# First layer item's projections, rotary products and GpSimd parts placed in the last two cross-attention iterations

## The reference

```
x = x + xattn(layernorm(x), ctx_768)            # 8 heads of 64, 77 context rows
h = layernorm(x)
for l in range(2):                               # 2 layers
    s = shift_token(h)                           # second half of the channels one token later
    q, k, v = split(s @ wqkv[l])                 # 256 -> 3 x 512
    q, k = l2norm(q) * qs, l2norm(k) * ks
    q, k = rotary_xpos(q, k)
    h = h + local_attention(q, k, v) @ wo[l]     # windows of 128, look back one window
    s = layernorm(shift_token(h)) * lg + lb
    a, g = split(s @ w1[l] + b1[l])
    h = h + (a * gelu(g)) @ w2[l] + b2[l]
x = x + h
```

## Time and profile before

| | us |
|---|---|
| median of 3 runs | 1458.46 |
| lowest and highest | 1457.38, 1459.85 |
| the profiled execution | 1456.24 |
| its span, first to last instruction | 1454.1 |
| mean granted TensorE clock | 0.995 |

### The profile page before, as it was taken

How to read it: one execution, slowest core, us unless ns; L and a number is a source line. 1 busy time by engine, 2 the same in 40 slices (tenths; PEclk the granted TensorE clock), 3 DMA queues, 4 the chain that set the end, 5 groups by cost and what they waited for, 6 DMA issues and landing times.

```text
span 1454.1 us, 32911 instructions
## 1 busy us (share of the span) xinstructions
PE 1404.0 (97%) x11652; PEld 1251.9 (86%) x11652; DVE 1099.9 (76%) x3067; ACT 936.7 (64%) x2662; POOL 761.4 (52%) x576
## 2 busy tenths in 40 slices
PE   7989999898999999999999999999999999999988
PEld 6888888787888888888888888888888888888877
DVE  5677677456888878777877878888778888887874
ACT  4777766345666666666666677666666666666662
POOL 1112112155666666665555667765566655555653
PEclk8999999999999999999999999999999999999999
DMA  6122111200001110000101021111111111111011
GB/s 211 39 95 100 46 59 45 103 16 19 29 29 29 29 29 28 28 28 28 31 29 30 27 69 36 32 50 37 36 37 36 35 35 35 35 35 35 29 36 31
DMA packets 50517, 63.43 MB, mean 44 GB/s; under 512 B 8402, under 2 KB 32104, under 8 KB 50408
## 3 DMA queue, kind: packets, MB, share of 16 engines
q1 hardware_dynamic: 50408, 61.99, 13.6%
HBM read 38.17 MB, written 16.78 MB: 38 GB/s over the span
## 4 chain that ended last, share of the span: by engine, by line
PE 66%; DVE 7%; issue 2%; POOL 2%; ACT 2%; DMA 1%; SPq 1%; DVEq 0%; ACTq 0%; POOLq 0%
PE pb L550 31%; PE pb L856 7%; PE pb L870 6%; PE pb L801 6%; PE pb L832 6%; PE pb L816 5%; PE pb L894 4%; DVE p_t L1533 1%; DVE p_t L1547 1%; DVE r_sin L1520 1%; DVE r_cos L1514 1%; DVE n_sq L1500 1%; POOL n_inv L1755 1%; ACT p_t L1171 1%; PE pb L760 1%
## 5 line engine op out<-in xcount | busy, mean ns | idle before, releaser
L1755 POOL TENSOR_TENSOR n_inv<-n_cl,half_neg 128x16 f32<-128x16 f32 x64 | 211.0, 3297 | 178.3 <-DVE n_cl L1505 174.8
L1171 ACT ACTIVATE p_t<-p_t,s_nm 128x128 f32<-128x128 f32 (+1 forms) x512 | 227.0, 448 | 17.3 <-DVE s_nm L1533 16.0
L550 PE MATMUL pb<-h_hi,w_hi 128*128 128x256 f32 x704 | 207.1, 294 | 0.8 <-DVE hg L1557 0.8
L550 PE MATMUL pb<-h_hi,w_lo 128*128 128x256 f32 x704 | 198.6, 282 | 0.0
L550 PE MATMUL pb<-h_lo,w_hi 128*128 128x256 f32 x704 | 198.6, 282 | 0.0
L1760 POOL TENSOR_TENSOR r_cos<-r_cos,r_sin 128x1024 f32<-128x1024 f32 x64 | 154.4, 2413 | 58.9 <-DVE r_sin L1520 58.9
L1162 ACT ACTIVATE pt_t<-pb 128x512 f32<-128x512 f32 x192 | 114.4, 597 | 100.8 <-PE pb L816 100.0
L1127 ACT ACTIVATE qk_sq<-pb 128x512 f32<-128x512 f32 x128 | 72.3, 591 | 156.1 <-PE pb L550 156.1
L1533 DVE CUSTOM_DVE_ANT_0 p_t<-pb,mask_t 128x128 f32<-128x128 f32 (+1 forms) x512 | 152.1, 354 | 25.8 <-PE pb L801 25.4
L1786 POOL TENSOR_TENSOR hg_lo<-hg,hg_hi 128x256 fp32r<-128x256 f32 (+1 forms) x192 | 142.4, 762 | 46.3 <-DVE hg_hi L1564 46.3
L550 PE MATMUL pb<-wqkv_hi,xt_hi 128*128 128x512 f32 x384 | 163.5, 426 | 2.1 <-DVE r_sin L1520 2.1
(11 more groups left out here) (145 smaller groups left out, 4052.9 us busy)
## 6 DMA issues: line engine op xcount, KB each, us to landing
y_state<-x SPq DMA_DIRECT2D x32, 256.0 KB, 2.1
x_cur<-y_state SPq DMA_DIRECT2D x32, 256.0 KB, 2.6
x_res<-y_state SPq DMA_DIRECT2D x32, 256.0 KB, 2.8
x_in<-x SPq DMA_DIRECT2D x16, 256.0 KB, 2.8
x_state<-x SPq DMA_DIRECT2D x16, 256.0 KB, 2.1
x_orig<-x_state SPq DMA_DIRECT2D x16, 256.0 KB, 2.9
out<-x SPq DMA_DIRECT2D x16, 256.0 KB, 2.2
x<-x SPq DMA_DIRECT2D x32, 112.0 KB, 2.3
```

What stands on the lines that cost most here:

```text
L550: mm = pe.matmul(dst, s, m, start=(n == 0 and k == 0), stop=(n == len(pairs) - 1 and k == 2))
L1171: e = nc.scalar.activation(pu, pu, ACT.Exp, bias=s_nm[:, j, k:k + 1], scale=-1.0, accum_out=s_sum[:, j, k:k + 1])
L1755: nc.gpsimd.tensor_tensor(n_inv[:, t], n_cl[:, t], half_neg[:], ALU.pow).then_inc(pool_inv, 1)
```

## The change

Item 0's chain is taken out of `run_l(0)` and put into `run_x(16)` and `run_x(17)`:

- **TensorE, g = 16**: `turn_x(0)` (into bank 4) right behind `x_out`; the three projections of the first half into banks 6, 5 and 7 behind `x_probs(15, 1)`, with a wait for GpSimd's two memsets of `xt` (`xt_zero`); ahead of `x_values(15)` a wait for the first `rotate` and the first copy of v, whose banks the values take. **g = 17**: the three projections of the second half, into banks 5, 4 and 2, ahead of `x_out(15)`. **Layer iteration 0**: only `turn_x(1)`, 56 idle products and `turn_qk(0)`, behind a wait for `x_residual(15)` (`x_res1`). The idle products of g = 16 and 17 (8, 14, 8 and 8) go, and the 5 and 18 of layer iteration 0.
- **ScalarE**: `x_hi(0)` ahead of the third group of exponentials of g = 16; squares and the copy of v ahead of the third copy of turned probabilities; the second half's at g = 17.
- **VectorE**: `x_lo(0)` behind `y_stats(14)`; `first_item(0)` (rotate, squares, clamp) ahead of `y_normed(14)`; `first_item(1)` at g = 17 ahead of `x_residual(15)`; `y_normed(15)` in layer iteration 0 behind `x_lo(1)`.
- **GpSimd**: the memsets of `xt` at the start of g = 16; `rotated(0, 0)` behind the deviation of sequence 14, `rotated(0, 1)` ahead of that of sequence 15. The other two memsets and `zero_made` stand behind both.
- **SP**: `x_cur` of item 1 is loaded at g = 16 behind the store of y 14, ahead of the stores of sequence 15.

```diff
+        FIRST_BANK = {(0, 0): 5, (0, 1): 6, (0, 2): 7, (1, 0): 4, (1, 1): 5, (1, 2): 2}
+        def is_first(n):
+            return isinstance(n, int) and n == 0
+        def qkv_bank(a, t, part):
+            return FIRST_BANK[t, part] if is_first(a) else part
+        def xt_bank(n):
+            return 4 if is_first(n) else 3
...
# SP, run_x, behind the stores of d
+                if g == SEQS:
+                    sp.wait_ge(pe_xt, 1)
+                    sp.dma_start(x_cur[:], one(y_dram, 1)).then_inc(cur_load, 16)
...
# TensorE, run_x
                 if g == SEQS + 1:
-                    turn_x(0)
-                if g >= SEQS:
-                    idle_products(8, 4)
+                    for part in (0, 1, 2):
+                        project(0, None, 1, part)
                 if d is not None:
                     x_out(a, d)
...
+                if g == SEQS:
+                    turn_x(0)
...
                     if g == SEQS:
-                        idle_products(14, 4)
+                        pe.wait_ge(xt_zero, 1)
+                        pe.wait_ge(w_lo, WEIGHT["w10c"])
+                        for part in (1, 0, 2):
+                            project(0, None, 0, part)
                     x_probs(b, 2)
-                    if g == SEQS:
-                        idle_products(8, 4)
                     x_probs(b, 3)
...
+                    if g == SEQS:
+                        pe.wait_ge(dve_rope, 1)
+                        pe.wait_ge(act_v, 1)
                     for t in range(NT):
                         x_values(b, was, t)
...
# TensorE, project
-                    if isinstance(a, int) and a == 0:
-                        pe.wait_ge(x_res1, SEQS)
-                    else:
+                    if not is_first(a):
                         pe.wait_ge(act_qkt, at(plus(a, -1), 4, 3 if part == 1 else 4))
...
# TensorE, run_l
                 if isinstance(g, int) and g == 0:
-                    idle_products(86, 7)
+                    idle_products(56, 7)
...
             def between(g):
                 if g == 0:
-                    pe.wait_ge(w_lo, WEIGHT["w10c"])
-                    pe.wait_ge(zero_made, 1)
+                    pe.wait_ge(x_res1, SEQS)
...
# ScalarE, run_x
+                if g == SEQS:
+                    x_hi(0)
                 if b is not None:
                     x_exps(b, 2)
                     x_exps(b, 3)
                     x_probs_copy(b, 0)
                     x_probs_copy(b, 1)
+                if g == SEQS:
+                    square(0, 0, 0)
+                    square(0, 0, 1)
+                    copy_v(0, 0, 0)
+                if g == SEQS + 1:
+                    square(0, 1, 0)
+                    square(0, 1, 1)
+                    copy_v(0, 1, 0)
...
# VectorE
+            def first_item(t):
+                rotate(0, t, 0)
+                squares(0, t)
+                clamp(0, t)
...
                 if g == SEQS + 1:
-                    x_lo(0)
+                    first_item(1)
                 if d is not None:
                     x_residual(d, par)
                     y_stats(d)
+                if g == SEQS:
+                    x_lo(0)
                 if b is not None:
                     x_maxes(b, 2)
...
+                if g == SEQS:
+                    dve.wait_ge(const_made, 2 * LAYERS)
+                    dve.wait_ge(x_bias, SEQS)
+                    first_item(0)
-                if d is not None:
+                if d is not None and d < SEQS - 1:
                     y_normed(d)
...
# VectorE, run_l
                 if has_next(a):
                     x_lo(plus(a, 1))
+                if is_first(a):
+                    y_normed(SEQS - 1)
...
# GpSimd, run_x
+                if g == SEQS:
+                    pool.wait_ge(x_pv, SEQS)
+                    nc.gpsimd.memset(xt_hi[:, T:T + 1].bitcast(F32), 0.0)
+                    nc.gpsimd.memset(xt_lo[:, T:T + 1].bitcast(F32), 0.0).then_inc(xt_zero, 1)
+                if g == SEQS + 1:
+                    rotated(0, 1)
                 if d is not None:
                     deviation(x_mv[:, 1, :, 1], x_ve[:, 1], x_rs[:, 1], d, y_bmv, d + 1, y_eps, y_rst)
+                if g == SEQS:
+                    rotated(0, 0)
...
+            def rotated(a, t):
+                add_parts(a, t)
+                inverse_norms(a, t)
+                norm_qk(a, t)
```

More of the change, by code:

```diff
@@ L509, in run_l @@
                 a, b, c, d, par = l_roles(g)
-                if has_next(a):
+                if has_next(a) and not is_first(a):
                     sp.wait_ge(pe_xt, at(a, 1, 1))
@@ L563, in turn_x @@
                     for t in range(NT):
[L564 removed]
+                        mm = pe.transpose(pb[:, xt_bank(n), c * T + t * P:c * T + t * P + P], x_cur[:, t, c * P:c * P + P], id_f)
                 mm.then_inc(pe_xt, 1)
@@ L911, in run_l @@
                     return
-                if isinstance(g, int) and g < 2:
+                if isinstance(g, int) and g == 1:
                     idle_products(5, 7)
@@ L915, in run_l @@
                     scores(a, b, 0)
-                if a is not None:
+                if a is not None and not is_first(a):
                     project(a, d, 0, 1)
-                if a is not None:
+                if a is not None and not is_first(a):
                     project(a, d, 0, 0)
@@ L928, in run_l @@
                     feed(c, d, 2)
-                if isinstance(g, int) and g < 2:
-                    idle_products(18 if g == 0 else 6, 7)
-                if a is not None:
+                if isinstance(g, int) and g == 1:
+                    idle_products(6, 7)
+                if a is not None and not is_first(a):
                     project(a, d, 1, 0)
@@ L1511, in rotate @@
                 half = DH // 2
-                qk = pb[:, 0:2].rearrange("p j (h d) -> p j h d", d=DH)
+                first = qkv_bank(a, t, 0)
+                qk = pb[:, first:first + 2].rearrange("p j (h d) -> p j h d", d=DH)
                 for j in range(2):
@@ L1824, in run_l @@
                     next_w1(2)
-                if a is not None:
-                    add_parts(a, 0)
-                    inverse_norms(a, 0)
-                    norm_qk(a, 0)
-                    add_parts(a, 1)
-                    inverse_norms(a, 1)
-                    norm_qk(a, 1)
+                if a is not None and not is_first(a):
+                    rotated(a, 0)
+                    rotated(a, 1)
                 if c is not None:
@@ L1839, in run_l @@
                     next_w2(0)
+            x_iterations(run_x)
+            nc.gpsimd.memset(x1[:, 0, 1], 0.0)
+            nc.gpsimd.memset(hg_hi[:, FC - 1].bitcast(F32), 1.0).then_inc(zero_made, 1)
             l_iterations(pool, run_l, lambda g: None)
```

33 lines of the change are left out of this document (11 added, 22 removed).

## The result

| | before | after |
|---|---|---|
| median us (6 runs each) | 1459.15 | 1451.04 |
| lowest, highest | 1457.38, 1461.76 | 1448.16, 1451.51 |
| ratio of the runs, 95% interval | | 0.9942 (0.9930 to 0.9954) |
| profiled execution, its span | 1456.24, 1454.1 | 1450.92, 1448.8 |
| scores of sequence 15 to `turn_qk(0)` | 256.19 to 301.34, 45.15 | 256.34 to 291.38, 35.04 |

The kernel became 8.1 us faster; 11.2 was forecast. The last two rows say where the rest went: 10.1 us were won in the handover, and behind it, where nothing was changed, the profiled execution is 4.6 us longer.

A forecast was written before the change was run, and what follows sets the result against it. TensorE was taken as the bound except in the handover, where it waits for others. `turn_qk(0)` at 290.1 instead of 301.34 is 11.2 us sooner; 1458.46 - 11.2 = 1447.3 us, range 1444.3 to 1451.0.

The forecast's parts named there:

- First projection: TensorE, g = 16: item 0's projections start at 265.25, after `x_lo` adds 0.7 us to an earlier wait.
- values: TensorE, g = 16: `x_values(15)` waits for the first rotate until 272.05, some 1.6 us idle.
- the clamp held to the end of the add: VectorE, g = 17: clamp lasts until 282.75 with GpSimd's add, delaying `x_residual(15)`; TensorE idles some 2 us.
- `turn_qk(0)` set by the filler and not by GpSimd: Layer iteration 0: 56 idle products end at 290.1, GpSimd at 287.7; `turn_qk(0)` comes 11.2 us sooner.
- The rule on the shared ports: Skill's exclusive VectorE-GpSimd lock, weighed and not followed for the power: `y_normed(14)` would wait, giving 1448.7 instead of 1447.3.
- The power did not hold VectorE: Answers a rival: GpSimd's power holds `y_normed(14)`, so the second rotate and all behind come 1.45 us later, 1448.7; chance 0.12.
- one fall: Rival: the clock falls once at the handover's pauses and costs 2 to 5 us, 1449.3 to 1452.4; chance 0.14.
- What removing the products cost: TensorE, g = 16: losing the idle products was said to cost nothing, since what they covered is waits.
- a clock under 1.00 between 257 and 325: Sign named in advance: a granted clock below full in this stretch of the trace makes the prediction wrong.
- From there I carry the gain through one for one: Behind `turn_qk(0)`: same program, paced by TensorE, so the whole 11.2 us reaches the end.
- I see no such transfer: Rival: something in the first layer iterations waits for a fixed time and gives the gain back, 1456 to 1461; chance 0.03.
- theory C: Formed after the result: q8 loads TensorE's code; with 182 fewer instructions its loads hit more shift transfers behind the handover.

The follow-up runs named there:

- fill34: The changed kernel with 34 instead of 56 idle products in layer iteration 0: 1447.02 us, ratio to the kernel before 0.9919.
- res_first: The changed kernel with `x_residual(15)` put between squares and clamp of the second half at g = 17: 1448.26 us, ratio to before 0.9920.
- control: The changed kernel run again, unaltered: 1449.99 us, ratio to the kernel before 0.9936.
- late_x: The changed kernel with item 1's `x_cur` load put back behind the store of x1 of sequence 15: 1455.86 us, ratio to before 0.9984.
- fill0: The changed kernel with no idle products in layer iteration 0: 1447.97 us, ratio to the kernel before 0.9931.
- before2: The kernel before, run once more unaltered for a second trace: 1457.35 us.
- idle12: The changed kernel with twelve idle products in TensorE's pause ahead of `x_values(15)` at g = 16: 1447.49 us, ratio to before 0.9922.
- best: The changed kernel with twelve idle products ahead of `x_values(15)` and 34 instead of 56 in layer iteration 0: 1445.75 us, ratio to before 0.9919.
- wide: Like best, but with 512-column products as filler, six for the twelve and sixteen for the 34: 1444.24 us, ratio to before 0.9907.
- covered: Like wide, plus eight more wide products in the pause ahead of `turn_x(1)`: 1445.03 us, ratio to before 0.9911.
- pad182: The changed kernel with 182 increments of an unused semaphore on TensorE's queue, at three places: 1463.12 us, ratio to before 1.0033.

## Why the prediction was right, and where it wasn't

The median of 1451.04 stands at the upper end of the range given (1451.0), 3.7 us above the forecast of 1447.3. Of that, 0.7 is the kernel before, which in these runs had 1459.15 instead of 1458.46. The path was right; two terms that the sum put at nothing, the clock and the shifts, were not nothing. That both together left the time there was partly luck, as the sum below shows.

**The path through the handover: right, step by step.** First projection forecast for 265.25, at 265.21; values for 272.05, at 272.04, released by `r_sin`; the clamp held to the end of the add, the residual behind it, 2.0 us of pause (2.01); `turn_qk(0)` set by the filler and not by GpSimd, 2.4 us forecast between the two, 2.3 found (289.05 against 291.38). fill34 and res_first showed both by experiment, 2.2 and 1.2 us.

**The rule on the shared ports.** `y_normed(14)` took 0.72 us, its usual length, and the power 3.01; I had put some 3.3. The power did not hold VectorE. The add does hold the clamp, twice in 1.31 us (0.72 us in res_first, where it starts later). The Trainium skill ("SBUF — State Buffer", section "SBUF: two separate sides") has the lock held for a whole instruction; the rows agree for the add and disagree for the power, and clamp and `y_normed(14)` are the same VectorE operation (TENSOR_SCALAR). That the power gives way by the length of the cast beside it was misread, though: powers without a cast beside them are as long in the kernel before (3.28 us at 359.62), and what lengthens one is not shown.

**The clock: the mechanism was named, its chance mis-sized.** I gave one fall 0.14 and left it out of the sum. In five of the six profiled executions that have the pause of 1.5 us uncovered (after, control, fill34, res_first, late_x; not fill0) it fell just behind it, and cost some 1.5 us: `turn_qk(0)` at 291.4 instead of 290.1 is this term. My evidence against was one pause of 3.58 us with no fall; before2 had the fall behind the same pause. One execution decides little. What removing the products cost was not nothing, as I wrote, but 1.5 us. In the four kernels with that pause covered (idle12, best, wide, covered; one execution each) it held there, and in best and wide it fell behind the next pause instead. By the prediction's own sign, a clock under 1.00 between 257 and 325, this part was wrong.

**"From there I carry the gain through one for one": wrong.** "I see no such transfer" is the sentence that failed. The shift of `x1` is one: VectorE waits some 1.3 to 1.6 us for it in every iteration but the last anyway (50.1 us in 32 waits in the trace of before), so what is added to its landing goes through. q8's packets, by theory C the loads of TensorE's code, moved against the program by 182 instructions, met it more often: 3.9 us in the mean of two traces each (1157.2 against 1153.3 from `turn_qk(0)` to the end).

**The sum.** Against the first trace of before the handover gives 45.15 - 35.04 = 10.1 us, less 4.6 behind it 5.5; the profiled executions are 5.3 apart. Against before2, whose clock fell in the handover too, it gives 46.72 - 35.05 = 11.7, less 3.4 (1157.2 against 1153.8) = 8.3; the medians are 8.1 and 9.1 apart. So part of the fall of the clock is not the change's: the kernel before has it as well in some executions, and the first trace, on which my sum stood, had been spared. How often each kernel has it stays open, since only profiled executions show it, and with it how the typical gain divides between the handover and the stretch behind. Ahead of the handover, where nothing was changed either, the scores start anywhere from 254.81 to 257.24 in these four traces, so such sums are good to a microsecond or two only.

**What is not shown.** That q8 carries TensorE's code follows from its moving when only TensorE's instructions changed, and from pad182, not from a name in the trace. In the table the stretch behind the handover goes with the instruction count, not strictly, and the block of 256 is an assumption that fits. The count alone was varied only once, by pad182, whose increments also delayed the handover. Why a given pause lets the clock fall and another doesn't is open.

## What to carry to other kernels

When work leaves a queue, its idle instructions go with it, and with them, by theory C, the alignment of the code loads: compare the stretches that weren't touched too, iteration by iteration, and look at which small transfers the path waits for. A filler has to be cut to the new wait (34 for 56 here gave 2.2 us), and a new wait on TensorE of even 1.5 us needs one (1.5 us), as does the next one: in best and wide the clock fell there instead. A cheap VectorE instruction that meets a long GpSimd addition isn't cheap (1.31 us here); what TensorE waits for goes in front of it.

The fastest kernel of these, wide, is 13.9 us below the kernel before by the medians (ratio 0.9907), and 4 to 5 us below the changed one, by that ratio against 0.9942 and 0.9936. Its interval overlaps those of best and covered, so which of the three is fastest is not shown.

## What the runs showed of the hardware

- With a packet of 16 KB on an instruction queue beside it, a transfer of 0.5 KB landed after 3.7 us instead of 1.7 (kernel after, item 5), and one of 15 KB after up to 3.6 instead of 2.1 (control).
- Increments of a semaphore on TensorE's queue take about 0.1 us each: 45 held the values for 3.2 us beyond the usual pause of 1.5 us, and 100 at the start put off its first product by 12 us. They are no cheap padding.
- Behind pauses of 1.5 to 5 us the granted clock was 0.50 for some 3 to 7 us in most executions and 1.00 in others, with the same instructions around.
